# Two attention layers on one core: the maximum scores contract over 64 rows for each half of the heads, in pairs on the two row halves of the array

## The reference, cut to what matters

```python
q = q.reshape(b, l, KVH, GROUPS, HD).transpose(0, 2, 3, 1, 4)
k = k.reshape(b, s, KVH, HD).transpose(0, 2, 1, 3)
scores = jnp.einsum('bkgld,bksd->bkgls', q, k) * scale
scores = scores + encoder_attention_mask[:, :, None, :, :]
attn = jax.nn.softmax(scores, axis=-1)
out = jnp.einsum('bkgls,bksd->bkgld', attn, v)
```

## Time and the profile before

| | |
|---|---|
| median of 3 runs | 980.55 us (980.52 to 983.88) |
| profiled execution | 982.06 us, of which the span is 980.3 us |
| busy: PE, DVE, POOL, ACT | 879.2, 720.9, 556.3, 469.2 us |
| mean granted clock of TensorE | 0.96 of full speed |

### The profile page before, as it was taken

How to read it: one execution, slowest core, us unless ns; L and a number is a source line. 1 busy time by engine, 2 the same in 40 slices (tenths; PEclk the granted TensorE clock), 3 DMA queues, 4 the chain that set the end, 5 groups by cost and what they waited for, 6 DMA issues and landing times.

```text
span 980.3 us, 18241 instructions
## 1 busy us (share of the span) xinstructions
PE 879.2 (90%) x5419; PEld 672.2 (69%) x5419; DVE 720.9 (74%) x1113; ACT 469.2 (48%) x998; POOL 556.3 (57%) x725
## 2 busy tenths in 40 slices
PE   6669989899898989989898998989999898998983
PEld 5566857768685775958667685775868677595741
DVE  4657686868868686886868678686876868678654
ACT  3636354554635455463544636354463545546240
POOL 6842574755558465564946557484555747454332
PEclk9979999999999999999999999999999999999987
DMA  7412232312222231232223213222322322113130
GB/s 262 124 29 52 74 88 69 82 60 74 65 80 67 82 87 54 59 86 80 64 75 89 62 54 91 80 64 64 78 65 71 85 81 70 54 48 81 35 92 22
DMA packets 47866, 73.35 MB, mean 75 GB/s; under 512 B 8800, under 2 KB 26848, under 8 KB 47712
## 3 DMA queue, kind: packets, MB, share of 16 engines
q1 hardware_dynamic: 47840, 73.03, 27.2%
HBM read 24.76 MB, written 8.39 MB: 34 GB/s over the span
## 4 chain that ended last, share of the span: by engine, by line
PE 76%; DVE 13%; issue 5%; ACT 4%; POOL 1%; DMA 1%; SPq 0%; POOLq 0%; ACTq 0%; DVEq 0%
PE wide L622 11%; PE den L718 6%; PE wide L679 6%; PE outt L718 6%; PE wide L703 4%; DVE mrow L1173 4%; PE gen L738 3%; PE gen L657 3%; PE gen L658 3%; PE gen L659 3%; PE gen L740 3%; PE gen L739 3%; DVE maxima L1162 3%; DVE mrow L1171 3%; PE wide L705 3%
## 5 line engine op out<-in xcount | busy, mean ns | idle before, releaser
L931 ACT ACTIVATE prob<-wide 128x512 f32<-128x512 f32 x256 | 143.1, 605 | 89.8 <-PE wide L703 70.5
L1162 DVE TENSOR_REDUCE maxima<-wide 128x4 f32<-128x512 f32 x256 | 168.7, 685 | 21.4 <-PE wide L679 17.4
L870 ACT ACTIVATE att<-wide,negmax 128x512 f32<-128x512 f32 x128 | 87.8, 687 | 122.6 <-DVE negmax L1106 122.5
L1185 DVE RECIPROCAL at<-den 128x512 f32<-128x512 f32 x32 | 107.3, 3353 | 23.0 <-PE den L718 23.0
L622 PE MATMUL wide<-ta,att 128*128 128x130 f32 x1024 | 117.0, 275 | 0.0
L622 PEld LDWEIGHTS wide<-ta,att 128*128 128x128 f32 x1024 | 115.6, 191 | 0.0
L463 POOL TENSOR_TENSOR ta<-ta,rowinv 128x520 f32<-128x520 f32 x32 | 33.8, 1057 | 137.7 <-DVE rowinv L1112 137.7
L456 POOL TENSOR_TENSOR ta<-ta,cb_s 128x772 f32<-128x772 f32 x64 | 106.7, 1700 | 6.5 <-ACT ta L878 4.4
L679 PE MATMUL wide<-kbh,qh 128*128 128x512 f32 x256 | 102.9, 447 | 0.8 <-DVE ql L1154 0.6
L703 PE MATMUL wide<-qstack,kstack 96*128 96x512 f32 (+1 forms) x256 | 97.3, 430 | 0.6 <-ACT att L870 0.5
L490 POOL TENSOR_TENSOR mv<-bns 128x4 f32<-128x4 f32 x16 | 3.3, 203 | 158.5 <-DVE bns L1206 158.5
(11 more groups left out here) (145 smaller groups left out, 2229.7 us busy)
## 6 DMA issues: line engine op xcount, KB each, us to landing
qstack<-qh SPq DMA_DIRECT2D x128, 128.0 KB, 2.3
xs<-in_x SPq DMA_DIRECT2D x16, 512.0 KB, 3.4
ys<-in_ctx SPq DMA_DIRECT2D x16, 512.0 KB, 3.8
kstack<-kbh SPq DMA_DIRECT2D x128, 64.0 KB, 2.0
qstack<-ql SPq DMA_DIRECT2D x64, 128.0 KB, 2.3
out_x<-late SPq DMA_DIRECT2D x32, 256.0 KB, 2.1
kstack<-kpl SPq DMA_DIRECT2D x64, 64.0 KB, 2.0
prob<-in_mask SPq DMA_DIRECT2D x1, 2048.0 KB, 10.8
```

The lines of the kernel that those rows point to most:

```text
L870: nc.scalar.activation(att[:, j, n], wide[:, slot(plan, f"en{j}{n}")], exp_f, bias=negmax[:, j, n:n + 1], accum_out=rowsum[:, j, n:n + 1]) ...
L931: nc.scalar.activation(prob[:, kv], wide[:, slot(plan, f"st{j}{kv}")], exp_f).then_inc(sem["prob_done"], 1)
L1162: nc.vector.tensor_reduce(maxima[:, j, at_head:at_head + 4], wide[:, slot(plan, f"mx{j}{g}{half}")].rearrange("p (b s) -> p b s", s=P), AX ...
L1185: nc.vector.reciprocal(at[:], den[:]).then_inc(sem["dinv_done"], 1)
```

## The change

For each half of the four query heads, the matmul takes only the 64 rows on which its keys are nonzero: rows 0 to 63 for `half` 0, rows 64 to 127 for `half` 1. The result is the same sum with the zero terms left out. The number of matmuls, their 512 columns and the PSUM tiles that they write stay. In the stretch after the first spread, the order on PE changes from one score and one maximum score in turn to two scores and then the two halves of a maximum score. In the rest of the kernel the two halves already follow each other. `WIDE_USES` is changed to the same order. The residual transpose of element 1 now comes after the first two scores instead of after the first. The streams of ACT, DVE, POOL and SP are unchanged.

```diff
-    + [u for kv in range(6) for u in ((f"st0{kv}", 2), (f"mx1{(kv + 2) // 2}{kv % 2}", 2))]
+    + [u for g in range(1, G) for u in ((f"st0{2 * g - 2}", 2), (f"st0{2 * g - 1}", 2), (f"mx1{g}0", 2), (f"mx1{g}1", 2))]
...
-                last = mm(o, qh[:, j, g], kbh[:, j, 4 * half:4 * half + 4], start=True, stop=not masked)
+                rows = slice(64 * half, 64 * half + 64)
+                last = mm(o, qh[rows, j, g], kbh[rows, j, 4 * half:4 * half + 4], start=True, stop=not masked)
...
-                    for kv in range(6):
-                        scores(q, plan, i, 0, kv, masked)
-                        if kv == 0:
+                    for g in range(1, G):
+                        scores(q, plan, i, 0, 2 * g - 2, masked)
+                        scores(q, plan, i, 0, 2 * g - 1, masked)
+                        if g == 1:
                             residual_transpose(q, plan, i, 1)
-                        max_scores(q, plan, i, 1, (kv + 2) // 2, kv % 2, masked)
+                        both_max_scores(1, g)
```

## The result

The changed kernel takes 1021.8 us (median of 4 runs, 1015.0 to 1027.5), the kernel before 982.0 us beside it. The ratio is 1.040, with a 95% interval from 1.033 to 1.048. The profiled execution is the fastest of the four: 1015.0 us, span 1013.1. So the trace shows 33 of the 40 us. In the changed kernel, lines behind L679 stand one or two lower: the maximum scores are L680, the spread L690, the residual copy L925, the two parts of the maxima L1173 (the CAST) and L1175.

A forecast was written before the change was run, and what follows sets the result against it. POOL's operations, not PE, were taken to set the spreads. Twelve turns at 11.16 us add 14.5 us and two more 1.6: 16.1 on 982.06 makes 998.2, less 1.5 to the median, 996.7 us; range 978 to 1008.

The forecast's parts named there:

- the chain: Behind the first spread: maxima end later, L1171 comes 0.45 us behind L463's start, second spread 11.16 us after first, not 9.53.
- POOL's steps: L1171 and L1173 on DVE finish only at an end of a POOL operation, in steps of 1.0 to 1.7 us.
- The first spread stayed put: Before the first spread: L1171 comes 0.26 us earlier, still behind POOL's step, so the spread starts when it did.
- The pairs of element 0: Three pairs ahead of the first spread: cheaper or dearer, they cost and bring nothing, hidden by POOL.
- `st01` waits for `en10`: Behind the first spread: `st01`'s bank is free only when ACT has done `en10` (540.02), so it starts at 540.07.
- the residual copy comes late: ACT's second residual copy, behind the first spread: 541.47 instead of 541.02; L463 follows it by 4.54 us.
- the stretch: First to second spread: 11.16 us in twelve turns, 10.65 in two whose clock doesn't fall; range 10.65 to 11.35.
- my sum: Whole kernel: twelve turns add 14.5 us, two more add 1.6, together 16.1; forecast 996.7 us, chance 0.61.
- Row tiles: Each pair on row halves: between 0.23 us gained and 0.42 lost; the gain was taken as likelier.
- The estimate from the rule: Each side-by-side pair: by skill rule and row together, about 0.2 us dearer than now (0.42 less 0.23).
- The clock: Pause before the first spread: grows from 2.55 to about 2.9 us, clock may fall sooner, 1 or 2 us in all.
- Rival 3: Before the second spread: L1171 falls behind L463's end, some 1.3 us later per turn, +17 more, 1014 us; chance 0.15.

The follow-up runs named there:

- e1: Only the 64-row slices, with the old order after the first spread, against the kernel before: 1.048 times its time (1.043 to 1.053); four runs, 1022.7 to 1053.0 us.

## Why the prediction was right and wrong

**Direction and the chain: right.** POOL's steps order the spreads (0.19 us for each part once the maxima lie in PSUM). The first spread stayed put. The pairs of element 0 changed nothing (1.002). `st01` waits for `en10`, the residual copy comes late, L463 with it, the CAST falls behind the start of L463, and L1175 ends with L472. I had 11.16 us for the stretch at the lower clock and 10.65 without; the turns at high clock show 10.80, and those of the order alone with 3.4 us of low clock 11.15 to 11.72. The order alone, which is what my sum priced, gave 1000.4 us where I had 996.7.

**Row tiles: priced at nothing.** I bounded a pair by 0.23 gained and 0.42 lost, read from the earlier trace rows that a change of tile costs 0.21 us on the way out, and then took the gain as likelier. The halves did run side by side, and the changes of tile ate more than that brought: +0.17 us. The estimate from the rule of the Trainium skill (TensorEngine Tiling (Array Packing), Key Properties) and the row, +0.2, was the right one. By time alone this error is small here, because POOL's steps hide it at the high clock: 10.80 us in the changed kernel, and 10.80 in the undisturbed turns of the order alone. With the steps gone it is 18 us. It also shortened the pause before the first spread, to 1.8 us, where I had forecast a growth to 2.9.

**The clock: the step that failed.** I priced it with "1 or 2 us for the longer pause, in which it may fall sooner". It cost about 25 us. I took the length of a low stretch from the earlier trace rows as given, and asked only where it would lie. Yet what PE does inside it changed. With the row tiles a low stretch lasted 13.7 us instead of 3.4 in four steady turns and in the first, and from 0.9 to 2.3 us behind the first spread on everything up to the second ran at 1.2 GHz: 13.96 us instead of 10.80, and 0.2 to 0.9 us more behind the second spread. Rival 3, the CAST behind the end of L463, came true in these turns, by this cause; I had it at 1014 us and from dearer pairs alone.

**Open.** Why the clock recovers after 3.4 us in one turn and after 13.7 or 17 in another, with PE busy in both, is told only in part: with changes of tile in the stream it gets longer, and half tiles or more changes seem to add to that. Nor is it known why it falls in only five of twelve steady turns of the changed kernel, and in none with the transpose put back. The length of the pause doesn't decide it: with 2.5 us the clock fell in all twelve steady turns of the kernel before but in three of twelve with the new order, 128 rows and the transpose back; with 1.8 us in five of the changed kernel, three of e1, two with the slices for element 0 alone, and none with the transpose back. With 0.8 us or less it fell in no steady turn. The low stretches of over 6.9 us in steady turns are all in kernels that have matmuls over 64 rows behind the pause.

## What to carry to other kernels

Two half-height matmuls side by side cost more here than two of full height, by 0.17 us for each pair that stands alone between full-width matmuls. So before packing, read the gap in front of and behind the tiles that are there, and charge it to every such pair. Whether packing pays where many pairs follow each other, no run here shows. When a low-clock stretch lies in the part that a change touches, its length is not a constant of the kernel; price also the case that it lasts through the whole of that part. And when a tiny DVE operation shows two lengths, look at what POOL runs beside it: moving its operand to PSUM gave 6% here, more than any order of the matmuls that was tried.

## What the hardware showed that I had not expected

The clock stayed at its lower level for up to 17 us (e1) while PE was busy for 16.87 of 16.95 us. Sixteen matmuls of 8 columns in another tile shape made a turn 2.7 us longer (60.67 against 57.9). And in the kernel before, keeping the clock up through the pause brought nothing at all (982.8 us against 980.8), because it put the CAST on the other side of a POOL step.
